# An attention loop with three turns in flight, its depthwise and output products in halves, and the next image's statistics beside qkv

## The chip, the core and the metric

The kernel runs on one core of one Trainium2 chip. The metric is the device time of one execution in microseconds (us). The engines are TensorE (PE: matmuls), VectorE (DVE), ScalarE (ACT), GpSimd (POOL) and SyncE (SP, which issues most transfers). Each engine runs its instructions in order; semaphores hold them together.

## The reference, cut to what matters

The kernel computes four layers on x of shape 8 x 128 x 56 x 56, each over a normalised input and added to it. The change touches only the first, attention over windows, once per image:

```python
xw = windows(x)                       # 7 x 7 windows of 8 x 8 pixels, 128 channels
proj = xw @ W_qkv + b_qkv             # q, k, v of 128 channels each
lepe = conv_general_dilated(v_img, lepe_w, padding='SAME', feature_group_count=C)  # 3 x 3 depthwise
logit = einsum('npc,nqc->npq', q_win * SCALE, k_win)      # window means
topk_logit, r_idx = top_k(logit, 4)
k_sel, v_sel = kv of the four chosen windows              # 256 keys for each window
attn = softmax(einsum('bmqc,bmkc->bmqk', q_h * SCALE, k_sel), axis=-1)   # 8 heads of 16
o = einsum('bmqk,bmkc->bmqc', attn, v_sel)
out = (o + lepe) @ W_o + b_o
```

## The kernel before

All images stay in SBUF (`X`). The eight images run one after the other (`B = 8`). For each, a qkv part makes q, k and v in seven blocks (`NBLK = 7`) of 448 pixels (`BLK`, 8 rows; `NWIN = 7` windows): ACT scales a block into `xb` (L1554), PE makes q, k, v and v by tokens (L1774 to L1782), ACT and DVE move them out of the banks, DVE sums windows (L1636). Then come the window logits, the search for the four best, and the transfer of the chosen indices (`row`, L1431). Depthwise blocks 0 and 1 run around the logits (L1800).

Then the attention loop over `P2 = 49` windows. In turn w the engines do, each in its order:

- PE (L1884 to L1888): `scores(w)` (L1829), four matmuls into banks 0 to 3, each waiting for the exponentials of the turn before (`s_ex`); `attend(w - 2)` (L1854), which waits for the copy `PT` (`s_Tc`), the gathered values (`s_vg`) and `s_o`; `turn(w - 1)` (L1842), eight transposes of the probabilities `Pr` into banks 4 and 5; `fill(w)`.
- ACT: `exps(w)` (L1567), `turned(w - 1)` (L1576), the copy to `PT`, and `fourth(w)`, the transfer of one of four value windows.
- DVE (L1722 to L1732): `maxes(w)` (L1666), the reciprocal of the first two sums (L1726), `between(w)`, the second reciprocal (L1729), and the fourth pair's normalising (L1731). `between(w)` holds `attended(w - 2)` (L1696, L1687), which joins the heads, and in some turns one more piece.
- POOL: `window(w + 2)` (L1494), the gather of keys, then `norm_first(w)` (L1504), the normalising of three pairs.
- SP: three of four value windows for each w (L1369), and `stack`, which lays rows for the depthwise product (L1398).

`fill(w)` on PE and `between(w)` on DVE share bank 7. The order is written out by hand in tables (L1299 to L1305). For block b: depthwise steps `lepe(b, dx)` at turns 7(b-2)+6, +7, +8; DVE's `copy_lepe(b)` (L1677) at 7(b-2)+9; the output product `out(b)` (L1811) at 7(b+1)+3; the output addition `add_out(b)` (L1671) at 7(b+1)+4 and `out_stats(b)` (L1682) a turn later. `out(b)` waits for `s_le` of block b+2, that is, for the copy; `lepe(b)` waits for `s_ev` of block b-3, that is, for the addition. The next image's statistics (`input_stats`, L1316) stand in turns 13, 15, 20, 22, 27, 29 and 30, and its mean and variance go over bank 7 in turns 33 and 40 (L1325, L1339, L1335).

```python
LEPE_AT = {NWIN * (b - 2) + 6 + dx: (b, dx) for b in range(2, NBLK) for dx in range(3)}
COPY_AT = {NWIN * (b - 2) + 9: b for b in range(2, NBLK)}
for w in range(2, P2):
    scores(w, w % 2)
    attend(w - 2, w % 2, (w - 2) % 3, (w - 2) // 3)
    turn(w - 1, (w + 1) % 2)
    fill(w)
```

Of the kernel before, what the change touches and what calls it, by code (L numbers as in the profile page):

```python
# [27 lines left out]
ACT = mybir.ActivationFunctionType  # L28
ALU = mybir.AluOpType
AXX = mybir.AxisListType.X  # L30
# [1108 lines left out]
def program(nc, a, out, last_stage=4):  # L1139
    root = ExitStack()  # L1140
    with root:
# [87 lines left out]
        with ExitStack() as c0:  # L1229
            sb, _, sem = mk(c0)  # L1230
            s_ldx = [sem("first_image_loaded"), sem("images_loaded")]
# [56 lines left out]
            Pr = sb("Pr", [C, 2, PAIRS, KEYS])  # L1288
# [3 lines left out]
            nmx = sb("nmx", [C, 2, PAIRS])  # L1292
            den = sb("den", [C, 2, PAIRS])
            rden = sb("rden", [C, 2, PAIRS])
# [77 lines left out]
            with nc.Block() as block:  # L1372
                @block.sync
                def _(sp):
# [9 lines left out]
                    for n in range(1, B):  # L1384
                        sp.dma_start(X[:, n * HW:(n + 1) * HW], x_in[n]).then_inc(s_ldx[1], 16)
# [83 lines left out]
                def _(pool):  # L1469
# [12 lines left out]
                    with pool.Fori(0, B) as n:  # L1482
# [15 lines left out]
                        def norm_first(w, par):  # L1498

                            for i, pairs in enumerate((slice(0, 2), slice(2, 3))):  # L1500
# [3 lines left out]
                                pool.tensor_tensor(Pr[:, par, pairs, :], Pr[:, par, pairs, :],  # L1504
                                                   rden[:, par, pairs].unsqueeze(2).to_broadcast([C, k, KEYS]), ALU.mult)\
# [4 lines left out]
                        with pool.Fori(0, (P2 - 3) // 2) as k:  # L1510
                            window(k * 2 + 2, 0)
                            norm_first(k * 2, 0)
                            window(k * 2 + 3, 1)
                            norm_first(k * 2 + 1, 1)
# [7 lines left out]
                def _(act):  # L1522
# [20 lines left out]
                    with act.Fori(0, B) as n:  # L1543
# [17 lines left out]
                        def exps(w, par):  # L1561

                            if not isinstance(w, int):
                                act.wait_ge(s_T, n * P2 + w)
# [45 lines left out]
                def _(dve):  # L1610
# [21 lines left out]
                    def image(n, more):  # L1632
# [343 lines left out]
```

## Time and profile before

| | us |
|---|---|
| median of 3 runs (3899.26 to 3907.92) | 3900.28 |
| profiled execution, its own time | 3898.74 |
| its span | 3897.0 |

The page's first two parts: busy time of each engine over the span, and the span in 40 slices of 97.4 us, in tenths.

```profile
PE 3509.7 (90%) x30516; PEld 2922.8 (75%) x30516; DVE 2500.8 (64%) x6153; ACT 2177.0 (56%) x5985; POOL 1837.3 (47%) x2998
...
PE   6989898888889898969999999999999968779998
...
DVE  4868687777868686853333333333333389989998
ACT  4878787887878787844443333333333334345554
POOL 2747374655647474720003333333334457756665
```

The attention layer is the first 17 slices or so. In the timeline an answer's line gives start, duration, engine, line of the kernel, operation, what it writes and reads, and how many instructions were merged; the brackets hold the idle time ahead of it and what ended it. A matmul of f32 data has two records.

### The profile page before, as it was taken

Reading aid. Unit: us, or ns where it says so; the run is one execution under the profiler, and the core shown is the slowest. Engines: PE = TensorE matmul, PEld = TensorE weight load, DVE = VectorE, ACT = ScalarE, POOL = GpSimd, SP = SyncE. Lnnn points to the kernel's source line nnn. Section 1 sums busy time; section 2 is a strip of 40 time slices with the busy share of each in tenths; the row PEclk is TensorE's granted clock in tenths of the full one; section 3 lists DMA queues with packets and bytes.
Section 4 is the critical chain, followed back from the end, with each engine's and each line's share of the span. In section 5 each row is a group of like instructions: output and inputs, shape, how many; then the busy total and the mean of one; then the engine's idle time right before and its main releaser. Section 6 shows DMA issues by size and latency. Waiting matters only on the chain. (4 is left out here: it accounts for less than half of the span.)

```text
span 3897.0 us, 106851 instructions
## 1 busy us (share of the span) xinstructions
PE 3509.7 (90%) x30516; PEld 2922.8 (75%) x30516; DVE 2500.8 (64%) x6153; ACT 2177.0 (56%) x5985; POOL 1837.3 (47%) x2998
## 2 busy tenths in 40 slices
PE   6989898888889898969999999999999968779998
PEld 3555555555555555559999999999999967779888
DVE  4868687777868686853333333333333389989998
ACT  4878787887878787844443333333333334345554
POOL 2747374655647474720003333333334457756665
PEclk9999999999999999989999999999999979989999
DMA  6232222223131323211110000000012100000000
GB/s 214 63 96 71 88 78 90 76 63 97 53 111 51 110 56 103 64 65 48 48 49 0 0 0 0 0 0 0 0 33 64 43 10 1 1 19 28 34 34 34
DMA packets 202728, 194.25 MB, mean 50 GB/s; under 512 B 35728, under 2 KB 190992, under 8 KB 199312
## 3 DMA queue, kind: packets, MB, share of 16 engines
q1 hardware_dynamic: 171024, 177.08, 14.6%
q10 hardware_dynamic: 31360, 12.87, 1.2%
q8 instruction: 181, 2.97, 0.3%
q14 instruction: 163, 1.34, 0.1%
HBM read 123.24 MB, written 66.58 MB: 49 GB/s over the span
## 5 line engine op out<-in xcount | busy, mean ns | idle before, releaser
L196 PE MATMUL bank<-h,w_hh 128*128 128x128 f32 x8032 | 933.8, 275 | 0.0
L196 PEld LDWEIGHTS bank<-h,w_hh 128*128 128x128 f32 x8032 | 917.1, 192 | 0.0
L1567 ACT ACTIVATE Pr<-bank,nmx 128x256 f32<-128x256 f32 x1568 | 721.0, 472 | 191.5 <-DVE nmx L1666 187.9
L241 ACT ACTIVATE h<-bank,bg 128x128 f32<-128x128 f32 x1008 | 370.0, 367 | 818.7 <-PE bank L196 818.6
L1504 POOL TENSOR_TENSOR Pr<-Pr,rden 128x512 f32<-128x512 f32 (+1 forms) x784 | 660.5, 853 | 182.6 <-DVE rden L1726 135.8
L1666 DVE TENSOR_REDUCE nmx<-bank 128x1 f32<-128x256 f32 x1568 | 553.8, 414 | 96.5 <-PE bank L1829 92.5
L1494 POOL COPY kg<-kT 128x64 f32 x1568 | 303.1, 237 | 535.0 <-DMA row<-ix 299.6
L287 DVE SCALAR_TENSOR_TENSOR inp<-bank,b_in,tz 128x256 f32<-128x256 f32 x196 | 85.8, 479 | 697.5 <-ACT tz L224 697.5
L260 POOL CAST h_hi<-h 128x512 fp32r<-128x512 f32 x196 | 119.7, 611 | 685.6 <-ACT h L241 685.6
L1829 PE MATMUL bank<-kg,qT 32*128 32x256 f32 x3136 | 410.3, 440 | 31.1 <-POOL kg L1494 22.3
L1576 ACT ACTIVATE PT<-bank 128x512 f32<-128x512 f32 x784 | 428.1, 609 | 15.9 <-PE bank L1842 15.7
L1842 PE MATMUL bank<-ident,Pr 128*128 128x128 f32 x3136 | 435.9, 283 | 0.0
L1842 PEld LDWEIGHTS bank<-ident,Pr 128*128 128x128 f32 x3136 | 341.9, 142 | 82.7 <-issue 73.3
L1854 PE MATMUL bank<-PT,vg 128*32 128x128 f32 x6272 | 265.2, 280 | 134.2 <-ACT PT L1576 129.9
L1829 PEld LDWEIGHTS bank<-kg,qT 32*128 32x128 f32 x3136 | 216.0, 189 | 225.5 <-ACT Pr L1567 155.8
L1854 PEld LDWEIGHTS bank<-PT,vg 128*32 128x32 f32 x6272 | 164.7, 110 | 281.1 <-issue 174.3
L970 POOL TENSOR_TENSOR v_ring<-points,v_ring 128x896 fp32r<-128x896 f32 x128 | 291.2, 2296 | 175.5 <-ACT v_ring L1000 175.5
L1567 ACT ACTIVATION_READ_ACCUMULATOR Pr<-bank,nmx 128x1 f32 x1568 | 318.0, 203 | 0.0
L661 PE MATMUL bank<-v_ring,u_hi 128*128 128x392 f32 x768 | 267.5, 348 | 52.7 <-POOL v_ring L970 52.7
L263 POOL TENSOR_TENSOR h_lo<-h,h_hi 128x512 fp32r<-128x512 f32 x196 | 251.6, 1284 | 35.3 <-POOL h_hi L260 35.3
L662 PE MATMUL bank<-v_ring,u_hi 128*128 128x392 f32 x768 | 262.9, 342 | 0.0
L663 PE MATMUL bank<-v_ring,u_lo 128*128 128x392 f32 x768 | 261.8, 341 | 0.0
(253 smaller groups left out, 6600.1 us busy)
## 6 DMA issues: line engine op xcount, KB each, us to landing
v_rows<-v_padded SPq DMA_DIRECT2D x168, 232.0 KB, 3.3
vg<-v_windows SPq DMA_DIRECT2D x1176, 32.0 KB, 2.1
first_gates<-gate_sums SPq DMA_DIRECT2D x28, 512.0 KB, 2.6
gate_sums<-first_gates SPq DMA_DIRECT2D x28, 512.0 KB, 3.6
v_padded<-vpad SPq DMA_DIRECT2D x56, 232.0 KB, 2.3
X<-in_x SPq DMA_DIRECT2D x8, 1568.0 KB, 15.1
vg<-v_windows ACTq DMA_DIRECT2D x392, 32.0 KB, 2.2
x_backup<-X SPq DMA_DIRECT2D x8, 1568.0 KB, 6.0
```

Source lines behind the costliest of these rows:

```text
L196: ins = pe.matmul(bank[m][:, tt * COLS:(tt + 1) * COLS], w_hh[:, k, m * 128:(m + 1) * 128], prev[:, k, :], start=False, stop=(k == NH - 1) ...
L241: act.activation(h[:, 2 * q + tt, m, :], bank[m][:, tt * COLS:(tt + 1) * COLS], ACT.Tanh, bias=bg[:, 0, m:m + 1]).then_inc(s_h, 1)
L661: pe.matmul(ps, w[0], x[0], start=first, stop=False)
L970: pool.tensor_tensor(halves(v[:, q % 3, 1], h), halves(pts, h), halves(v[:, q % 3, 0], h).bitcast(F32), ALU.subtract).then_inc(s_lo, 1)
L1494: ins = pool.tensor_copy(kg[:, par, r * W2:(r + 1) * W2], kT[:, bass.ds(i * W2, W2)])
L1504: pool.tensor_tensor(Pr[:, par, pairs, :], Pr[:, par, pairs, :], rden[:, par, pairs].unsqueeze(2).to_broadcast([C, k, KEYS]), ALU.mult)\
L1567: act.activation(Pr[:, par, j, :], bank[j][:, 0:KEYS], ACT.Exp, bias=nmx[:, par, j:j + 1], accum_out=den[:, par, j:j + 1])\
L1576: act.activation(PT[:, par, i * 512:(i + 1) * 512], bank[4 + i][:], ACT.Copy)\
L1666: dve.tensor_reduce(nmx[:, par, j:j + 1], bank[j][:, 0:KEYS], AXX, ALU.max, negate=True)\
L1829: pe.matmul(bank[j][:, 0:KEYS], qT[32 * j:32 * j + 32, w, :], kg[32 * j:32 * j + 32, par, :], start=True, stop=True).then_inc(s_S, 1)
L1842: ins = pe.transpose(bank[4 + j // 2][:, (j % 2 * 2 + c) * C:(j % 2 * 2 + c + 1) * C], Pr[:, par, j, c * C:(c + 1) * C], ident[:])
L1854: ins = pe.matmul(bank[6][32 * j:32 * j + 32, 0:C], vg[:, slot, c, 32 * j:32 * j + 32], PT[:, par, (2 * j + c) * C:(2 * j + c + 1) * C], s ...
```

## The change

The attention loop gets one more turn in flight: `Pr`, `nmx`, `den` and `rden` become rings of three, PE attends w-3 and turns w-2 beside scores w, ACT copies w-2, DVE joins w-3. The 448-column depthwise and output products are cut into halves of 224 columns; `FILL_AT` gives each half its turn: output halves at 7(b+1)+3 and +4, depthwise halves at 7(b-2)+5, +6, +7, +8 (two) and +9. The copy moves to 7(b-2)+10 and `ADD_LAG` to 5. The next image's seven bn_stats move out of the loop, one behind each qkv block; its aggregate to turn 6, the mean's product to turn 40 and the variance's to 41, with DVE's parts a turn later each. The second image's load gets a semaphore of its own. Block 2's rows are stacked from window 2 on. Loops of POOL and ACT are unrolled by six for the rings of three.

```diff
-            s_ldx = [sem("first_image_loaded"), sem("images_loaded")]
+            s_ldx = [sem("first_image_loaded"), sem("second_image_loaded"), sem("images_loaded")]
...
-            Pr = sb("Pr", [C, 2, PAIRS, KEYS])
+            Pr = sb("Pr", [C, 3, PAIRS, KEYS])
...
-            OUT_LAG, ADD_LAG = 3, 4
-            STATS_AT = {13: 0, 15: 1, 20: 2, 22: 3, 27: 4, 29: 5, 30: 6}
-            MEAN_AT, VAR_AT = 33, 40
-
-            LEPE_AT = {NWIN * (b - 2) + 6 + dx: (b, dx) for b in range(2, NBLK) for dx in range(3)}
-            COPY_AT = {NWIN * (b - 2) + 9: b for b in range(2, NBLK)}
-            STACK_AT = {3: 2, 8: 3, 12: 4, 18: 5, 25: 6}
+            ADD_LAG = 5
+            MEAN_AT, VAR_AT = 40, 41
+
+            HALF = BLK // 2
+            FILL_AT = {w: [] for w in range(P2)}
+            for b in range(NBLK - 1):
+                for h in range(2):
+                    FILL_AT[NWIN * (b + 1) + 3 + h].append(("out", b, 0, h))
+            for b in range(2, NBLK):
+                for i, w in enumerate((5, 6, 7, 8, 8, 9)):
+                    FILL_AT[NWIN * (b - 2) + w].append(("lepe", b, i // 2, i % 2))
+            COPY_AT = {NWIN * (b - 2) + 10: b for b in range(2, NBLK)}
+            STACK_AT = {2: 2, 8: 3, 12: 4, 18: 5, 25: 6}
...
-                        window(P2 - 1, 0)
-                        norm_first(P2 - 3, 0)
-                        norm_first(P2 - 2, 1)
-                        norm_first(P2 - 1, 0)
+                        with pool.Fori(0, (P2 - 2) // 6) as k:
+                            for i in range(6):
+                                window(k * 6 + i + 2, i % 2)
+                                norm_first(k * 6 + i, i % 3)
...
+                            if not (isinstance(w, int) and w < 3):
+                                act.wait_ge(s_T, n * P2 + w - 1)
...
+                        def turn_window(w, i):
+                            exps(w, (i + 2) % 3)
+                            turned(w - 2, i % 2)
+                            fourth(w - 1, (i + 1) % 3)
...
+                            if more:
+                                if b == 0:
+                                    dve.wait_ge(s_ldx[1], 16)
+                                input_stats(dve, following(n), b)
...
-                            if w >= 2:
-                                attended(w - 2)
+                            if w >= 3:
+                                attended(w - 3)
...
+                            if more and w == NWIN - 1:
+                                dve.wait_ge(s_ldx[2], 16 * (B - 2))
                                 input_aggregate(dve, following(n))
-                            if more and w == MEAN_AT:
+                            if more and w == MEAN_AT + 1:
                                 input_mean(dve, following(n))
-                            if more and w == VAR_AT:
+                            if more and w == VAR_AT + 1:
                                 input_var(dve, following(n))
...
+                                ins = pe.matmul(to[STRIP * i:STRIP * i + STRIP, h * HALF:(h + 1) * HALF],
+                                                w_tap[:, dx * STRIPS + i, :],
+                                                vrow[:, b % 2, i, h * ROWS // 2:(h + 1) * ROWS // 2, dx:dx + W],
+                                                start=(dx == 0 and h == 0), stop=(dx == 2 and h == 1))
...
+                        def out(b, h):
+                            if h == 0:
+                                pe.wait_ge(s_o, n * P2 + (b + 1) * NWIN + 1)
+                                if b + 2 < NBLK:
+                                    pe.wait_ge(s_le, n * NBLK + b + 3)
+                                else:
+                                    pe.wait_ge(s_ev, n * NBLK + b + 1)
+                            ins = pe.matmul(bank[7][:, h * HALF:(h + 1) * HALF], w_o[:],
+                                            by_row(oT[:, b % 2, :])[:, h * ROWS // 2:(h + 1) * ROWS // 2],
+                                            start=(h == 0), stop=(h == 1))
...
+                            for what, b, dx, h in FILL_AT[w]:
+                                if what == "out":
+                                    if more and b == NBLK - 2 and h == 0:
+                                        pe.wait_ge(s_id, following(n) * IN_DVE + 4)
+                                    out(b, h)
+                                else:
+                                    if dx == 0 and h == 0:
+                                        if b == 2:
+                                            pe.wait_ge(s_le, n * NBLK + 2)
+                                        else:
+                                            pe.wait_ge(s_ev, n * NBLK + b - 1)
+                                    lepe(b, dx, h, bank[7])
                             if more and w in (MEAN_AT, VAR_AT):
-                                pe.wait_ge(s_ev, n * NBLK + b + 2)
+                                pe.wait_ge(s_ev, n * NBLK + (w - NWIN) // NWIN + 2)
...
-                        for w in range(2, P2):
+                        for w in range(3, P2):
                             scores(w, w % 2)
-                            attend(w - 2, w % 2, (w - 2) % 3, (w - 2) // 3)
-                            turn(w - 1, (w + 1) % 2)
+                            attend(w - 3, (w - 3) % 2, (w - 3) % 3, (w - 3) // 3)
+                            turn(w - 2, (w - 2) % 3)
                             fill(w)
```

## Rows read from the trace of the kernel before

**Rows 1.** The timeline (start us, us, engine, line, operation), DVE: marks of turns 0, 20, 27, 48.
```profile
275.00 0.17 DVE L1726 RECIPROCAL rden<-den 128x2 f32<-128x2 f32 x1
...
341.30 0.17 DVE L1726 RECIPROCAL rden<-den 128x2 f32<-128x2 f32 x1
...
364.78 0.17 DVE L1726 RECIPROCAL rden<-den 128x2 f32<-128x2 f32 x1
...
434.95 0.17 DVE L1726 RECIPROCAL rden<-den 128x2 f32<-128x2 f32 x1
```

**Rows 2.** The timeline, second image, turns 13 to 15, PE and ACT.
```profile
319.18 0.62 ACT L1576 ACTIVATE PT<-bank 128x512 f32<-128x512 f32 x1
...
320.05 0.67 PE L1854 MATMUL bank<-PT,vg 128*32 128x128 f32 x16 [0.28 <-ACT PT L1576]
...
321.67 0.96 PE L1800 MATMUL bank<-v_rows,w_tap 96*32 96x448 f32 x8
...
322.56 0.71 PE L1829 MATMUL bank<-kg,qT 32*128 32x256 f32 x8
...
323.75 0.47 ACT L1567 ACTIVATE Pr<-bank,nmx 128x256 f32<-128x256 f32 x1 [0.60 <-DVE nmx L1666]
...
325.56 0.61 ACT L1576 ACTIVATE PT<-bank 128x512 f32<-128x512 f32 x1
```

**Rows 3.** The timeline, second image, turns 9 and 10.
```profile
303.83 0.47 ACT L1567 ACTIVATE Pr<-bank,nmx 128x256 f32<-128x256 f32 x1 [0.81 <-DVE nmx L1666]
...
305.59 0.61 DVE L1677 COPY lepe<-bank 128x448 f32<-128x448 f32 x1
...
307.03 0.47 ACT L1567 ACTIVATE Pr<-bank,nmx 128x256 f32<-128x256 f32 x1 [0.30 <-DVE nmx L1666]
...
308.31 0.92 PE L1811 MATMUL bank<-oT,w_o 128*128 128x448 f32 x2
```

**Rows 4.** Idle time by releaser (us, times): PE ahead of L1842, PE ahead of L1854.
```profile
  POOL Pr L1504: 9.4, 29
...
  ACT PT L1576: 231.5, 445
```

**Rows 5.** The timeline, end of the second image's loop.
```profile
435.71 1.09 ACT L1576 ACTIVATE PT<-bank 128x512 f32<-128x512 f32 x2
...
436.86 0.67 PE L1854 MATMUL bank<-PT,vg 128*32 128x128 f32 x16 [1.25 <-ACT PT L1576]
...
438.59 1.08 ACT L1576 ACTIVATE PT<-bank 128x512 f32<-128x512 f32 x2 [1.78 <-PE bank L1842]
```

**Rows 6.** The timeline, marks of turns 0, 1 and 2 of the third image.
```profile
483.40 0.17 DVE L1726 RECIPROCAL rden<-den 128x2 f32<-128x2 f32 x1
...
486.43 0.17 DVE L1726 RECIPROCAL rden<-den 128x2 f32<-128x2 f32 x1
...
490.14 0.17 DVE L1726 RECIPROCAL rden<-den 128x2 f32<-128x2 f32 x1
```

**Rows 7.** Busy time by stretch; the third number from the end is the granted clock.
```profile
486.00:488.00 2.00, 2.00 (x15) 1.56 (x13) 1.13 (x5) 1.82 (x8) 1.77 (x6) 0.50 0.16 44
```

**Rows 8.** The timeline: output addition, input statistics, then the mean in turn 33.
```profile
312.09 0.68 DVE L1671 SCALAR_TENSOR_TENSOR X<-bank,cb,X 128x448 f32 x1
...
318.63 0.62 DVE L1316 BATCH_NORM_STATS2 bn_in<-X 128x6 f32 x1
...
384.21 0.47 ACT L1567 ACTIVATE Pr<-bank,nmx 128x256 f32<-128x256 f32 x1 [0.23 <-DVE nmx L1666]
...
385.76 0.28 PE L1325 MATMUL bank<-input_norm,group 128*128 128x1 f32 x2
...
386.85 0.22 DVE L1335 SCALAR_TENSOR_TENSOR input_norm<-input_norm 128x1 f32<-128x1 f32 x1
```

**Rows 9.** The timeline, DVE in a qkv block before the third image's loop.
```profile
459.25 0.68 DVE L1642 TENSOR_SCALAR kT<-bank,vec 128x448 f32<-128x448 f32 x1 [1.52 <-PE bank L1775]
```

**Rows 10.** The images' loads from in_x: time from issue to landing.
```profile
DMA to landing us min/median/max: 6.7/15.1/26.3
```

More of the change, by code:

```diff
@@ L1509, in _ @@
                         window(1, 1)
[L1510 to L1514, printed above, removed]
-                        window(P2 - 1, 0)
-                        norm_first(P2 - 3, 0)
-                        norm_first(P2 - 2, 1)
-                        norm_first(P2 - 1, 0)
+                        with pool.Fori(0, (P2 - 2) // 6) as k:
+                            for i in range(6):
+                                window(k * 6 + i + 2, i % 2)
+                                norm_first(k * 6 + i, i % 3)
+                        for w in range((P2 - 2) // 6 * 6, P2):
+                            if w + 2 < P2:
+                                window(w + 2, w % 2)
+                            norm_first(w, w % 3)
                     pool.wait_ge(s_S, (B * P2 + 1) * PAIRS)
@@ L1599, in _ @@
                         exps(0, 0)
-                        with act.Fori(0, (P2 - 1) // 6) as k:
-                            for i in range(6):
-                                exps(k * 6 + i + 1, (i + 1) % 2)
-                                turned(k * 6 + i, i % 2)
-                                fourth(k * 6 + i + 1, (i + 1) % 3)
-                        turned(P2 - 1, 0)
+                        exps(1, 1)
+                        def turn_window(w, i):
+                            exps(w, (i + 2) % 3)
+                            turned(w - 2, i % 2)
+                            fourth(w - 1, (i + 1) % 3)
+                        exps(2, 2)
+                        turned(0, 0)
+                        fourth(1, 1)
+                        with act.Fori(0, (P2 - 3) // 6) as k:
+                            for i in range(1, 7):
+                                turn_window(k * 6 + i + 2, i)
+                        for w in range((P2 - 3) // 6 * 6 + 3, P2):
+                            turn_window(w, w - 2)
+                        turned(P2 - 2, (P2 - 2) % 2)
+                        fourth(P2 - 1, (P2 - 1) % 3)
+                        turned(P2 - 1, (P2 - 1) % 2)
                         with act.If(n < B - 1):
@@ L1792, in image, with lepe @@
                         pe.wait_ge(s_v, n * NBLK + NBLK)
-                        def lepe(b, dx, to):
-                            if dx == 0:
+                        def lepe(b, dx, h, to):
+                            if dx == 0 and h == 0:
                                 loads = 4 - b % 2
@@ L1814, in image @@
-                        for dx in range(3):
-                            lepe(0, dx, bank[7])
+                                ins = pe.matmul(to[STRIP * i:STRIP * i + STRIP, h * HALF:(h + 1) * HALF],
+                                                w_tap[:, dx * STRIPS + i, :],
+                                                vrow[:, b % 2, i, h * ROWS // 2:(h + 1) * ROWS // 2, dx:dx + W],
+                                                start=(dx == 0 and h == 0), stop=(dx == 2 and h == 1))
+                            if dx == 2 and h == 1:
+                                ins.then_inc(s_lp, 1)
@@ L1816, in image @@
+                        for i in range(6):
+                            lepe(0, i // 2, i % 2, bank[7])
                         pe.wait_ge(s_k, n * NBLK + NBLK)
@@ L1818, in image @@
                         pe.matmul(bank[1][0:P2, 0:P2], qs[:], ks[:], start=True, stop=True).then_inc(s_lg, 1)
-                        for dx in range(3):
-                            lepe(1, dx, bank[6])
+                        for i in range(6):
+                            lepe(1, i // 2, i % 2, bank[6])
                         pe.wait_ge(s_tk, n * 3 + 2)
@@ L1830, in scores, with turn @@
                                           start=True, stop=True).then_inc(s_S, 1)
-                        def turn(w, par):
+                        def turn(w, tri):
                             pe.wait_ge(s_nF, (n * P2 + w) * 2 + 1)
```

81 lines of the change are left out of this document (29 added, 52 removed).

## The prediction

> **What bounds the kernel now.** I read the page's first two parts, then how one line that runs once per turn is spaced, then one image's loop in order of time. Per image there are 49 windows, one turn each: PE writes scores, DVE takes maxima, ACT exponentiates, POOL and DVE normalise, PE turns the probabilities, ACT copies them, PE attends. DVE's first reciprocal (L1726) marks the turn. In the second image the marks run from 275.00 to 434.95: 48 turns in 159.95 us [rows 1]. All that is changed lies in this first stage, eight images long.
>
> No engine is full in the loop, so I look for rings of waits. E(w) is the start of ACT's exponentials of turn w.
>
> Ring one goes over two turns [rows 2]: a copy to PT ends at 319.80, attend starts at 320.05 (+0.25), the fill behind attend and turning at 321.67 (+1.62), the next scores at 322.56 (the fill, +0.89), exponentials at 323.75 (+1.19), the next copy at 325.56 (+1.81), and it takes 1.09 [rows 5]. The first step is 0.06 where a copy starts at 435.71 and attend at 436.86 [rows 5]; the mean I take is 0.18. Without its fill the ring is 0.18 + 1.62 + 1.19 + 1.81 + 1.09 = 5.89: E(w+1) is not before E(w-1) + 5.89 + the fill of turn w.
>
> Ring two goes over one turn, between ACT and DVE: exponentials at 303.83 and 307.03, 3.20 apart, where DVE has a depthwise copy of 0.61 in the turn [rows 3]. I take 3.2 also for turns with an output addition (0.68) or output statistics (0.62, as the row of the input's), [rows 8]. Without such work it is 3.03 (marks 483.40 and 486.43) [rows 6].
>
> With d(w) = E(w+1) - E(w): d(w) is the larger of ring two and 5.89 + fill - d(w-1). Turns 20 to 26 come out at 3.58, 3.2, 3.58, 3.2, 3.53, 3.2, 3.2 = 23.5; measured 364.78 - 341.30 = 23.48 [rows 1]. The two rules carry the loop.
>
> **Three turns in flight.** PE's order was scores(w), attend(w-2), turning(w-1); it becomes scores(w), attend(w-3), turning(w-2). ACT's was exponentials(w), copy(w-1); it becomes exponentials(w), copy(w-2). Before and after, PE in turn w waits for the copy that ACT made in turn w-1, and ACT in turn w copies what PE turned in turn w. Both rings keep their steps and lengths. What gets a turn more room is the normalising, between exponentials and turning, and it has room now: PE waited 9.4 us for POOL's probabilities in the whole kernel, 29 times in 392 turns [rows 4]. I take nothing for it; 9.4 is the most.
>
> The deeper loop drains longer. A stage of attend, turning and copy takes 2.9 us (copies start at 435.71 and 438.59 [rows 5]), and there is one more: +2.9 per image. At the start turn 1 takes 3.71 now (486.43 to 490.14 [rows 6]), since turning(0) stands ahead of scores(2); it moves behind, and ring two alone is left: 3 x 3.03 = 9.1 for turns 0 to 2, some 0.8 less. But TensorE's granted clock there is 0.50, the 1.2 GHz level [rows 7], after a stretch with little work, and the new order has still less work for PE at that place, so a turn more may run at it: bounds 0 and +1.4 (turning, attend and scores at twice their time, less what ring two hides); I take +0.6, between them, as nothing decides.
>
> **Halves.** A depthwise step of 448 columns adds 0.89; its row says 0.96, so the end overlaps by 0.07, and the output product's 0.92 [rows 3] adds 0.85. A half adds at least half: 0.445 and 0.42. It is eight records of 224 columns. Scores' eight of 256 take 0.71, attend's sixteen of 128 take 0.67, with the same 32-column weights as here [rows 2]. By scores a half is 0.61; by a straight line between attend (0.042 less the overlap) and the full step (0.111) it is 0.48. I take 0.48 and 0.44 for the weights' form. The Trainium skill would have it near the lower end: "TensorE: Matmul & The Clock Gate", section on the back-to-back issue gap, has a gap of columns over clock and some 2.5 ns, so a cut costs next to nothing; by that the sum is some 6 us less, and no row here has such a half.
> In seven turns there were four fills, 3.5 us; there are eight halves, 3.76, two of them in one turn. Were that all, turns would even out to 3.34, 3.2, 3.17, 3.68, 3.03, 3.30, 3.03 = 22.75 for 23.5.
>
> **The new waits.** Here the change hurts. In the kernel before each buffer goes from DVE to PE with a turn between: lepe(2) is copied by DVE in turn 9 (305.59), output product 0 runs on PE in turn 10 (308.31) [rows 3]. After the change the copy of block b is at 7(b-2)+10, and the output product of block b-2, which waits for it (s_le) as both use bank 7, at 7(b-1)+3: the same number. Likewise the first depthwise step of block 3 is in turn 12 and waits (s_ev) for output addition 0, which ADD_LAG 5 puts in turn 12. DVE comes to this work 1.76 after E(w) and ends at +2.37 (copy) or +2.44 (addition) [rows 3, 8]; PE is ready at +1.28 (308.31 for E = 307.03 [rows 3]). PE runs in order: behind the waiting fill stand scores(w+1), and behind those DVE's maxima and ACT. So d = 2.37 + 0.1 + 0.44 + 1.19 = 4.1 with a copy and 2.44 + 0.1 + 0.48 + 1.19 = 4.2 with an addition, 0.1 being the wake-up (between 0.06 and 0.25 above). Copies fall on turns 10, 17, 24, 31, 38, additions on 12, 19, 26, 33: nine turns per image. A period is 4.2 + 3.2 + 3.17 + 3.68 + 3.03 + 4.1 + 3.03 = 24.4, for 23.5.
>
> **The next image's statistics.** Seven bn_stats of 0.62 [rows 8] leave the loop for the qkv blocks, one each. There DVE idles 1.52 per block behind PE's k product [rows 9], so 0.9 is left over; where DVE starts an image late it has made that up after two blocks. I take 0; if the cover fails, 7 x 0.6 per image. DVE's wait for image 1 stands ahead of the first image's window sums and so of ACT: issued at 7.0 as the first of seven, landing 6.7 to 26.3 later [rows 10], likely before qkv starts, at worst some 10 us once.
> The mean's product moves from turn 33 to 40, where PE must first wait for output addition 4, in turn 40 as well: 2.44 + 0.1 + 0.2 + 1.19 = 3.93, 0.2 being the product (0.28 in its row). The variance's product in turn 41 waits for the mean's chain, which ends 2.86 after E (384.21, 386.85 + 0.22): 2.86 + 0.1 + 0.2 + 1.19 = 4.35 [rows 8].
> Depthwise blocks 0 and 1 are in halves too. Block 0 stands ahead of the logits: 6 x 0.48 for 3 x 0.89, +0.2; block 1 lies beside the search for the four best and their transfer. SP stacks block 2's rows a window earlier and PE wants them a turn earlier; the last goes out behind window 3's gathers, two turns ahead of its use. SP's gathers and ACT's fourth keep their distance to attend. Nothing for these.
>
> **The sum, an image with a next one.** Turns 0 to 4: 9.1 + 3.6 + 3.0 = 15.7. Turns 5 to 11: 3.34, 3.03, 3.34, 3.51, 3.03, 4.1, 3.03 = 23.4. Turns 12 to 39: 4 x 24.4 = 97.6. Turns 40 to 47: 3.93, 4.35, 3.15, 3.03, 3.03, 3.30, 3.03, 3.2 = 27.0. Together 163.7 for 159.95: +3.8. Drain +2.9, block 0 +0.2: +6.9, seven times: +48. The last image has neither statistics nor the waits of the norm, before or after; I put it at +6. In all +54 us on the profiled execution's 3898.74: 3953 us. The median of the runs stands 1.5 above that execution, which I leave to the range.
>
> **The rivals.**
> *A, the waits are met (the other side: faster).* If DVE's copy or addition is done when PE comes to the fill, the nine turns fall back to 3.3 (-7.5) and the two of the norm to 3.2 (-1.9): -2.5 per image with the drain, 3880 us in all. It decides at one point: whether PE reaches the fill earlier or later than 2.4 after E(w). It is there at 1.28, so against it. Partly met (3893 to 3906) is no change.
> *B, the third turn takes away PE's wait ahead of attend.* PE idled 231.5 us there behind ACT's copy [rows 4]. A gap that repeats can come from too few buffers, and then turns would fall to ring two's 3.03: 48 x 3.03 = 145.4, +3.1, so -11.4 per image, some 3807 us. Against it: what ends this gap is ACT's copy of the turn before, in the new order as in the old. (The Trainium skill, "Perfetto Trace Analysis", section on the optimization strategy, reads consistent bubbles so.)
> *C, halves at the scores' rate, 0.61.* +0.13 for each of four waiting fills, half of that for some 20 others, 0.8 on block 0: +2.6 per image, 3974 us.
> *D, the low clock lasts* a turn more at the start and falls in the longer drain, where turning and attend then take twice their time: +2 per image, 3970 us.
>
> **How the numbers follow.** Forecast 0.64; A 0.06, partly met 0.06; B 0.03; C 0.11; D 0.10. Low end: each wait 0.2 cheaper (9 x 8 x 0.2 = 14) and no slow turn at the start (5): 3932. High end: C with half of D: 3985. Left out are A, B and their like, 0.15, and little above. The measurement can tell 0.2%, 8 us, from no change. Faster 0.09 (A, B), same 0.06, slower 0.85.
>
> **What would show it.** The marks L1726 4.1 to 4.2 apart in turns 10, 12, 17, 19, 24, 26, 31, 33 and 38, 3.9 in 40, 4.4 in 41, and 3.0 to 3.2 in most others; PE idle ahead of the output product and the first depthwise half, ended by DVE's copy and addition; three copies after the last exponentials; blocks of qkv no longer than before. It is wrong if those turns take 3.3, or the others fall well below 3.0 or rise above 3.4.

## The result

| | before | after |
|---|---|---|
| median of 4 runs each, us | 3900.13 (3899.26 to 3907.92) | 3968.29 (3965.46 to 3972.22) |
| profiled execution, its own time | 3898.74 | 3965.46 |
| its span | 3897.0 | 3963.6 |
| loop, turn 0 to turn 48, mean of images 0 to 6 | 159.99 | 164.29 |
| loop of the last image | 156.15 | 160.07 |
| last mark to the next image's first, mean of seven | 48.11 | 51.77 |

The ratio is 1.0171, 95% interval 1.0153 to 1.0189: slower, by 68 us where 54 were forecast. A mark is, as before, DVE's first reciprocal of a turn; it stands in L1744 now. "Turn w" is from mark w to mark w+1. The loops and gaps in this table and in all that follow are worked out from the 392 marks of a trace.

The span's +66.6 splits so: seven loops 7 x 4.30 = 30.1, the last loop 3.9, seven gaps 7 x 3.67 = 25.7, the first mark 0.9 later (68.12 for 67.23), 3.1 between the last mark and the next layer's first product L196, and 2.9 behind it, where the change touches nothing.

The page's first part: no engine got much more work.

```profile
PE 3521.4 (89%) x31972; PEld 2970.5 (75%) x31972; DVE 2482.8 (63%) x6153; ACT 2180.1 (55%) x5985; POOL 1831.1 (46%) x2998
```

PE has 12 us more busy time and DVE 18 us less than before. So most of the 68 us is not added work; it comes from the order. The timeline of the second image, turns 10 and 12 (start us, us, engine, line, operation, what it writes and reads; in brackets the idle time ahead of it and what ended it):

```profile
315.98 0.47 ACT L1572 ACTIVATE Pr<-bank,nmx 128x256 f32<-128x256 f32 x1
...
317.66 0.61 DVE L1698 COPY lepe<-bank 128x448 f32<-128x448 f32 x1
...
318.42 0.62 PE L1833 MATMUL bank<-oT,w_o 128*128 128x224 f32 x2 [0.55 <-DVE lepe L1698]
...
318.97 0.82 PE L1854 MATMUL bank<-kg,qT 32*128 32x256 f32 x8
...
320.16 0.47 ACT L1572 ACTIVATE Pr<-bank,nmx 128x256 f32<-128x256 f32 x1 [1.17 <-DVE nmx L1687]
...
323.11 0.47 ACT L1572 ACTIVATE Pr<-bank,nmx 128x256 f32<-128x256 f32 x1
...
324.77 0.68 DVE L1692 SCALAR_TENSOR_TENSOR X<-bank,cb,X 128x448 f32 x1
...
325.58 0.59 PE L1819 MATMUL bank<-v_rows,w_tap 96*32 96x224 f32 x8 [0.57 <-DVE X L1692]
...
327.28 0.47 ACT L1572 ACTIVATE Pr<-bank,nmx 128x256 f32<-128x256 f32 x1 [1.15 <-DVE nmx L1687]
```

In turn 10 the exponentials start at 315.98 and the next ones at 320.16: 4.18. One follows the chain through four engines. DVE ends the copy at +2.29, PE starts the output half at +2.44, scores at +2.99, and the next exponentials start at +4.18. Behind PE's 0.55 us of waiting ACT idles 1.17 for DVE's maxima: a wait on one engine is handed round. In the kernel before, the same product had the turn to itself [rows 3] and scores didn't wait. Turn 12 is the same with the addition and the first depthwise half, 4.17.

The groups by line tell how often over the whole kernel (busy us, mean ns, then the idle time ahead and what ended it):

```profile
L1819 PE MATMUL bank<-v_rows,w_tap 96*32 96x224 f32 x2688 | 172.0, 360 | 24.9 <-DVE X L1692 20.5 <-ACT vst L1543 4.5
...
L1833 PE MATMUL bank<-oT,w_o 128*128 128x224 f32 x224 | 66.9, 389 | 33.8 <-DVE lepe L1698 27.9 <-DVE oT L1708 5.9
```

The rows hold what is new: 20.5 us ended by the addition and 27.9 by the copy. The view of L1833 puts the 27.9 down to 40 waits, five copies in each of eight images.

Turn 41 of the same image, where the variance's product waits for the mean's chain:

```profile
426.59 0.22 DVE L1341 SCALAR_TENSOR_TENSOR input_norm<-input_norm 128x1 f32<-128x1 f32 x1
...
426.87 0.38 PE L1345 MATMUL bank<-input_norm,group 128*128 128x1 f32 x2 [1.48 <-DVE input_norm L1341]
...
428.37 0.47 ACT L1572 ACTIVATE Pr<-bank,nmx 128x256 f32<-128x256 f32 x1 [1.43 <-DVE nmx L1687]
```

This wait has a second price, in some images only. In the first, third and seventh image TensorE's granted clock falls to the 1.2 GHz level right behind it, and turn 42 takes 4.02 to 4.06 us where it takes 2.95 in the other four with a next image. The third image, PE behind the variance's product, and the windows around it (the third number from the end is the granted clock):

```profile
643.97 0.38 PE L1345 MATMUL bank<-input_norm,group 128*128 128x1 f32 x2 [1.40 <-DVE input_norm L1341]
...
646.14 1.97 PE L1867 MATMUL bank<-ident,Pr 128*128 128x128 f32 x8
```

```profile
642.00:644.00 2.00, 0.60 (x7) 0.36 (x5) 1.79 (x9) 2.00 (x8) 1.43 (x4) 1.00 0.11 31
...
646.00:648.00 2.00, 2.00 (x12) 1.57 (x8) 1.68 (x8) 1.41 (x7) 1.68 (x6) 0.50 0.06 16
```

The eight transposes take 1.97 us there; in the second image, with the same wait of 1.48 and the clock at 1.00, they take 1.09.

The end of the loop (its last mark is 448.19), which answers to [rows 5], and the first two qkv blocks of the next image:

```profile
450.32 0.67 PE L1879 MATMUL bank<-PT,vg 128*32 128x128 f32 x16 [1.49 <-ACT PT L1581]
...
456.26 0.67 PE L1879 MATMUL bank<-PT,vg 128*32 128x128 f32 x16 [1.38 <-ACT PT L1581]
...
461.57 1.86 PE L1793 MATMUL bank<-PT,w_qkv 128*128 128x448 f32 x2 [2.05 <-ACT PT L1559]
...
463.23 1.70 PE L1794 MATMUL bank<-PT,w_qkv 128*128 128x448 f32 x2
...
466.21 1.87 PE L1801 MATMUL bank<-w_qkv,PT 128*128 128x128 f32 x8
...
468.01 1.02 PE L1793 MATMUL bank<-PT,w_qkv 128*128 128x448 f32 x2
```

Three attends behind the last mark (the first and the last are shown) where there were two: the last starts 8.07 us after it, before 4.98 (439.93 after the mark at 434.95, [rows 1]). That is +3.09. And in this gap the whole first qkv block runs at the 1.2 GHz level: its four products take 6.44 us (461.57 to 468.01), where the one before had its third and fourth at full rate, 1.15 and 1.19, and took 5.25 (445.22 to 450.47). The windows show the clock:

```profile
456.00:458.00 2.00, 1.01 (x17) 0.77 (x18) 0.89 (x4) 1.49 (x3) 0.00 (x0) 0.87 0.01 4
458.00:460.00 2.00, 1.52 (x4) 0.83 (x3) 1.21 (x7) 0.53 (x1) 0.00 (x0) 0.50 0.05 12
...
466.00:468.00 2.00, 2.00 (x9) 1.40 (x7) 0.39 (x1) 0.00 (x0) 0.00 (x0) 0.57 0.04 17
...
500.00:502.00 2.00, 1.19 (x5) 1.19 (x6) 1.32 (x5) 1.80 (x8) 1.12 (x5) 0.50 0.13 36
...
510.00:512.00 2.00, 2.00 (x22) 1.62 (x15) 1.68 (x7) 1.89 (x8) 1.40 (x5) 0.50 0.06 16
512.00:514.00 2.00, 1.27 (x19) 0.73 (x21) 1.39 (x5) 1.26 (x3) 1.13 (x3) 0.98 0.17 48
```

By these shares the first low stretch runs from about 457.5 to 467.7, after a drain in which PE was idle for nearly half of the time, and the second to 512.1, past the mark of turn 3 (511.01). The seven gaps differ: the first qkv block takes 4.99 to 6.44 us (mean 5.99), where it took 4.93 to 5.29 (mean 5.12) before.

### The profile page after: what moved, and what is told of

Same layout as the page of the kernel before. It is cut to its first block and busy times, and to the rows that moved or that the text cites. A ratio compares the mean times of both kernels' runs of the same rounds, so it can differ in the third digit from the quotient of the medians.

```text
span 3963.6 us, 108732 instructions
## 1 busy us (share of the span) xinstructions
PE 3521.4 (89%) x31972; PEld 2970.5 (75%) x31972; DVE 2482.8 (63%) x6153; ACT 2180.1 (55%) x5985; POOL 1831.1 (46%) x2998
## 3 DMA queue, kind: packets, MB, share of 16 engines
q8 instruction: 194, 3.18, 0.3%
## 5 line engine op out<-in xcount | busy, mean ns | idle before, releaser
L196 PE MATMUL bank<-h,w_hh 128*128 128x128 f32 x8032 | 933.8, 275 | 0.0
L196 PEld LDWEIGHTS bank<-h,w_hh 128*128 128x128 f32 x8032 | 917.0, 192 | 0.0
L1510 POOL TENSOR_TENSOR Pr<-Pr,rden 128x512 f32<-128x512 f32 (+1 forms) x784 | 658.2, 853 | 157.6 <-DVE rden L1744 140.1
L1854 PE MATMUL bank<-kg,qT 32*128 32x256 f32 x3136 | 380.2, 448 | 34.5 <-POOL kg L1500 22.1
L1854 PEld LDWEIGHTS bank<-kg,qT 32*128 32x128 f32 x3136 | 199.2, 192 | 172.6 <-ACT Pr L1572 86.1
```

The source lines that it names most:

```text
L196: ins = pe.matmul(bank[m][:, tt * COLS:(tt + 1) * COLS], w_hh[:, k, m * 128:(m + 1) * 128], prev[:, k, :], start=False, stop=(k == NH - 1) ...
L1510: pool.tensor_tensor(Pr[:, tri, pairs, :], Pr[:, tri, pairs, :], rden[:, tri, pairs].unsqueeze(2).to_broadcast([C, k, KEYS]), ALU.mult)\
L1854: pe.matmul(bank[j][:, 0:KEYS], qT[32 * j:32 * j + 32, w, :], kg[32 * j:32 * j + 32, par, :], start=True, stop=True).then_inc(s_S, 1)
```

## The experiments

Each kernel was timed in several rounds beside the kernel before on the same chip, in four groups: the kernel before came out at 3900.13, 3904.02, 3901.60 and 3901.53. So when times of different groups are set side by side, up to 4 us can be the group's. All results in one table (loop and gap as above; "period" is turns 12 to 18, the sum of their medians over images 0 to 6; "in flight" the turns). Loops and gaps are of the one profiled execution, which lies up to 5.9 us off its kernel's median (x6_cut and x5_two 5.9 and 5.3 above, x1_gaps and x3_sooner 5.4 and 5.0 below):

| kernel | in flight | us | beside before | ratio (95%) | loop | period | gap |
|---|---|---|---|---|---|---|---|
| before | 2 | | | | 159.99 | 23.48 | 48.11 |
| after | 3 | 3968.29 | 3900.13 | 1.0171 (1.0153 to 1.0189) | 164.29 | 24.29 | 51.77 |
| x1_gaps | 3 | 3920.43 | 3904.02 | 1.0043 (1.0026 to 1.0060) | 158.49 | 23.03 | 51.79 |
| x2_addgap | 3 | 3958.83 | 3904.02 | 1.0137 (1.0120 to 1.0154) | 163.32 | 24.05 | 51.61 |
| x3_sooner | 3 | 3924.46 | 3904.02 | 1.0053 (1.0036 to 1.0070) | 159.00 | 23.28 | 51.91 |
| x4_three | 3 | 3928.14 | 3904.02 | 1.0060 (1.0043 to 1.0077) | 159.29 | 23.40 | 52.34 |
| x8_undo3 | 2 | 3952.54 | 3901.60 | 1.0126 (1.0108 to 1.0144) | 165.52 | 24.95 | 49.28 |
| x6_cut | 2 | 3900.88 | 3901.60 | 1.0000 (0.9990 to 1.0009) | 160.38 | 23.49 | 48.38 |
| x7_stats | 2 | 3904.14 | 3901.60 | 1.0012 (1.0003 to 1.0022) | 159.87 | 23.48 | 48.22 |
| x5_two | 2 | 3894.13 | 3901.60 | 0.9978 (0.9968 to 0.9988) | 158.96 | 23.13 | 49.07 |
| x9_late | 2 | 3893.76 | 3901.53 | 0.9977 (0.9968 to 0.9986) | 158.15 | 23.12 | 48.73 |
| x10_both | 3 | 3911.46 | 3901.53 | 1.0022 (1.0013 to 1.0031) | 157.61 | 23.03 | 51.42 |

### The waits: x1_gaps, x2_addgap, x3_sooner

The theory: the nine turns of 4.2 come from hand-overs over bank 7 that DVE and PE have in the same turn. Three ways to take them away, each on the kernel after.

x1_gaps gives each hand-over its turn again, with all else kept:

```diff
-            ADD_LAG = 5
+            ADD_LAG = 4
-                    FILL_AT[NWIN * (b + 1) + 3 + h].append(("out", b, 0, h))
+                    FILL_AT[NWIN * (b + 1) + 3].append(("out", b, 0, h))
-                for i, w in enumerate((5, 6, 7, 8, 8, 9)):
+                for i, w in enumerate((5, 6, 6, 7, 7, 8)):
-            COPY_AT = {NWIN * (b - 2) + 10: b for b in range(2, NBLK)}
+            COPY_AT = {NWIN * (b - 2) + 9: b for b in range(2, NBLK)}
```

> The changed kernel with a turn between every hand-over of bank 7: depthwise halves in turns +5, +6, +6, +7, +7, +8, copy at +9, both output halves in one turn, addition a turn later; three turns in flight and the statistics beside qkv stay. Theory (the nine same-turn waits): no turn of 4.18 is left but turn 41; a period of seven turns falls from 24.3 to 23.2, the mean's wait goes, 6 us less per image: about 3920 us. Rival (the time comes from the third turn, the halves or the clock, not from the waits): the time stays at 3968.

x2_addgap takes away the additions' four alone; the copies' five stay:

```diff
-                for i, w in enumerate((5, 6, 7, 8, 8, 9)):
+                for i, w in enumerate((6, 6, 7, 8, 8, 9)):
```

> The changed kernel with only the first depthwise half a turn later (turns +6, +6, +7, +8, +8, +9): the four waits for the output addition go, the five for the copy stay. Theory: turns 12, 19, 26, 33 fall from 4.17 to 3.2, turns 10, 17, 24, 31, 38 stay at 4.18; a period falls by 0.6 as the halves crowd in two turns; about 3950 us. Rival: no change, 3968.

x3_sooner keeps the tables and turns DVE's order round, so that the copy or addition is ready earlier:

```diff
-                            if w >= 3:
-                                attended(w - 3)
                             b, lag = divmod(w - NWIN, NWIN)
                             if w in COPY_AT:
                                 copy_lepe(COPY_AT[w])
                             if b >= 0 and lag == ADD_LAG:
                                 add_out(b)
+                            if w >= 3:
+                                attended(w - 3)
```

> The changed kernel with DVE doing the copy or the addition before the two attended steps of the same turn, so that it ends 0.54 us sooner after the exponentials; all tables as they are. Theory (PE waits for DVE's piece in the same turn): the nine turns of 4.18 and turn 40 each fall by 0.54, 5.4 per image, about 3925 us. Rival: the same work in another order on DVE, no change, 3968.

The groups of the depthwise and output products by line, first x1_gaps, then x2_addgap, then x3_sooner:

```profile
L1819 PE MATMUL bank<-v_rows,w_tap 96*32 96x224 f32 x2688 | 163.7, 359 | 5.1 <-ACT vst L1543 5.1
...
L1833 PE MATMUL bank<-oT,w_o 128*128 128x224 f32 x224 | 52.9, 359 | 5.9 <-DVE oT L1708 5.9
```

```profile
L1819 PE MATMUL bank<-v_rows,w_tap 96*32 96x224 f32 x2688 | 163.7, 359 | 6.0 <-ACT vst L1543 6.0
...
L1833 PE MATMUL bank<-oT,w_o 128*128 128x224 f32 x224 | 64.9, 378 | 32.1 <-DVE lepe L1698 26.2 <-DVE oT L1708 5.9
```

```profile
L1819 PE MATMUL bank<-v_rows,w_tap 96*32 96x224 f32 x2688 | 172.0, 360 | 9.0 <-ACT vst L1543 4.2 <-DVE X L1692 3.6
...
L1833 PE MATMUL bank<-oT,w_o 128*128 128x224 f32 x224 | 64.9, 378 | 12.4 <-DVE lepe L1698 6.0 <-DVE oT L1708 5.9
```

In x1_gaps both kinds of wait are gone, and with them the mean's in turn 40 (3.96 to 3.09), and so are 48 of the 68 us (3920.43; 52, each kernel beside its own kernel before). Turn 41 is 4.27, no other median over 3.8. In x2_addgap "DVE X" is gone and "DVE lepe" stays at 26.2, in the places foretold: turns 12, 19, 26 and 33 fell from 4.17 to 3.17 to 3.40, turns 10, 17, 24, 31 and 38 kept 4.18. But the time fell by 9 us only (13, each beside its own kernel before): turns 13 and 15 rose from 3.09 and 3.61 to 3.76 and 3.92. What a turn is spared is partly paid in the next ones, as ring one goes over two turns. A small part is the clock: the low stretch behind turn 41 comes in six images of x2_addgap (turn 42 at 3.41 to 4.04) and in three of the kernel after, some 2 us more. So the kinds don't add up: the nine together with the mean's wait are worth 48 us, the four alone 9.

In x3_sooner the work is the same in the same turns, only 0.6 us earlier. Its turn 10, in the second image:

```profile
310.12 0.17 DVE L1744 RECIPROCAL rden<-den 128x2 f32<-128x2 f32 x1
...
310.20 0.62 DVE L1698 COPY lepe<-bank 128x448 f32<-128x448 f32 x1
...
310.97 0.62 PE L1833 MATMUL bank<-oT,w_o 128*128 128x224 f32 x2
...
313.76 0.17 DVE L1744 RECIPROCAL rden<-den 128x2 f32<-128x2 f32 x1
```

The copy starts 0.08 after the mark for 0.62, the output half 0.85 for 1.38, and the turn takes 3.64 for 4.18: what the copy gains, the turn gains. Turn 41, whose wait is not touched, stays at 4.33. So the length of these turns hangs on when DVE is done.

### Three turns in flight: x4_three, x8_undo3

x4_three has three in flight alone: whole products in the old turns (the copy at +9, ADD_LAG 4), the statistics in the loop as before. x8_undo3 is the other way round, the kernel after with two in flight:

```diff
-                            attend(w - 3, (w - 3) % 2, (w - 3) % 3, (w - 3) // 3)
-                            turn(w - 2, (w - 2) % 3)
+                            attend(w - 2, w % 2, (w - 2) % 3, (w - 2) // 3)
+                            turn(w - 1, (w + 1) % 2)
```

> The kernel before with three turns in flight alone: whole products, the old tables, statistics in the loop. Theory: the loop's turns stay as before, each image pays the longer drain (+3.1) and some 1.5 of low clock behind it: about 3928 us. Rival (the third turn takes away PE's wait ahead of attend): well below 3900.

> The changed kernel without its third turn: rings of two, attend w-2, turning w-1, but the changed tables with their same-turn waits, halves and statistics beside qkv. Theory (third turn worth +24 to +29, waits the rest): the turns of 4.18 stay, the drain is one stage shorter; about 3941 us. Rival (the third turn softens the waits): above 3968.

x4_three is +24 us beside its kernel before, as foretold. The first and last of the three attends in its drain (last mark 437.30), and the wait ahead of attend in its whole kernel:

```profile
439.50 0.67 PE L1878 MATMUL bank<-PT,vg 128*32 128x128 f32 x16 [1.49 <-ACT PT L1582]
...
445.43 0.67 PE L1878 MATMUL bank<-PT,vg 128*32 128x128 f32 x16 [1.38 <-ACT PT L1582]
```

```profile
  ACT PT L1582: 240.3, 457
```

The gap from image to image is 4.2 us longer, the loop 0.7 shorter. Of the 4.2 the drain is 3.1: in every gap of all kernels with three in flight the last attend starts 8.04 to 8.13 us behind the last mark, with two in flight 4.97 to 5.00. The first qkv block adds 0.7 (mean 5.82 for 5.12). PE's wait for PT is 240.3 us, for 231.5 [rows 4]: a third buffer does nothing for a bubble that ends with the copy of the turn before.

x8_undo3 came out at 3952.54, 11 over the 3941 expected: taking three in flight away gives back some 17 us of 68 (16 by the medians alone), and the waits cost no less with two turns in flight: the loop is even 1.2 longer. The nine turns are 4.24 to 4.26 there. The expectation had the loop unchanged by the turns in flight; in all four pairs (x4_three with before, after with x8_undo3, x10_both with x9_late and with x5_two) three in flight shortens it, by 0.7, 1.2, 0.5 and 1.3 us per image, and lengthens the gap, by 4.2, 2.5, 2.7 and 2.4. In the last three pairs the gap grows by less than the drain's 3.1: their kernels with two in flight have longer first qkv blocks (means 5.74, 5.80 and 5.73) than the kernel before (5.12). Why the low clock falls otherwise there was not found. Which wait the third turn relieves was not found: PE's wait for POOL's probabilities is 9.4 us before and 10.4 in x4_three.

### The cut and the statistics alone: x6_cut, x7_stats

x6_cut is the kernel before with every product in two halves, both in the turn of the whole one:

```diff
+            for b in range(NBLK - 1):
+                for h, w in enumerate((3, 3)):
+                    FILL_AT[NWIN * (b + 1) + w].append(("out", b, 0, h))
+            for b in range(2, NBLK):
+                for i, w in enumerate((6, 6, 7, 7, 8, 8)):
+                    FILL_AT[NWIN * (b - 2) + w].append(("lepe", b, i // 2, i % 2))
```

> The kernel before with every depthwise and output product cut in two, both halves in the old turn. Theory from the changed kernel's rows (two halves back to back take 0.90 for 0.89): the cut itself costs nothing, 3901 to 3906 us. Rival (a half at 0.48 alone, or at the scores' rate 0.61): 3910 to 3950.

3900.88, ratio 1.0000, and a period of 23.49 for 23.48: the cut costs nothing. The timeline of the kernel after shows why (last image: one half, the scores behind it, and in the next turn two halves):

```profile
1699.35 0.59 PE L1819 MATMUL bank<-v_rows,w_tap 96*32 96x224 f32 x8
...
1699.87 0.71 PE L1854 MATMUL bank<-kg,qT 32*128 32x256 f32 x8
...
1702.44 0.96 PE L1819 MATMUL bank<-v_rows,w_tap 96*32 96x224 f32 x16
```

Two halves one behind the other take 0.90 (1702.44 to the next scores at 1703.34), the whole step took 0.89 [rows 2]; a half alone delays scores by 0.52; why that is more than half of the whole was not run apart. The Trainium skill, "TensorE: Matmul & The Clock Gate", section on the back-to-back issue gap, gives the gap between isolated matmuls at the full clock as columns over the clock and some 2.5 ns. By that a cut costs next to nothing, an estimate from the page's figure, and for halves that stay together the run agrees: 3900.88 for 3901.60.

x7_stats is the kernel before with the statistics alone moved: seven bn_stats into the qkv blocks, the mean's product in turn 40, the variance's in 42.

```diff
-            STATS_AT = {13: 0, 15: 1, 20: 2, 22: 3, 27: 4, 29: 5, 30: 6}
-            MEAN_AT, VAR_AT = 33, 40
+            MEAN_AT, VAR_AT = 40, 42
```

> The kernel before with only the next image's statistics moved beside qkv, and its mean's and variance's products in turns 40 and 42, each with a turn between. Theory: qkv's blocks stay at 3.48, turns 30, 33 and 35 of the loop fall from 3.7 to 3.1, so 1.9 less per image: about 3890 us. Rival (the cover in qkv fails): 7 x 0.6 more per image, 3920 or more.

The expectation was wrong: 3904.14, ratio 1.0012, for 3890. The cover in qkv held (the gap is 48.22 for 48.11), but the loop is 0.12 shorter, not 1.9. By the medians, turns 13, 15, 20, 22, 27 and 29, from which a bn_stats had gone, did not move by more than 0.01: what DVE did there had held up nothing. Turns 30 and 33 gained (3.74 to 3.21, 3.69 to 3.18), but turn 31 rose from 2.95 to 3.31 and turn 34 from 3.03 to 3.48; the sums of turns 26 to 32 and 33 to 39 are 0.16 and 0.18 lower, and that of 40 to 47 is 0.31 higher. Turn 41 shows by what:

```profile
412.62 0.17 DVE L1726 RECIPROCAL rden<-den 128x2 f32<-128x2 f32 x1
...
413.32 0.15 DVE L1329 COPY input_norm<-bank 128x1 f32<-128x1 f32 x1
...
414.06 0.22 DVE L1334 SCALAR_TENSOR_TENSOR input_norm<-input_norm 128x1 f32<-128x1 f32 x1
...
414.51 0.17 DVE L1729 RECIPROCAL rden<-den 128x2 f32<-128x2 f32 x1 [0.23 <-issue]
...
416.48 0.17 DVE L1726 RECIPROCAL rden<-den 128x2 f32<-128x2 f32 x1
```

The mean's three steps (the first and the last are shown) stand between the two reciprocals, 413.32 to 414.28, and the second one comes 1.89 after the first. The turn is 3.86.

### What is left: x5_two, x9_late, x10_both

x5_two is two in flight with all the rest: halves in the old order but spread (5, 6, 6, 7, 7, 8), statistics in qkv, products of the norm in turns 40 and 42.

> Two turns in flight, halves spread with a turn between every hand-over (+5, +6, +6, +7, +7, +8, copy +9, output in one turn, addition a turn later), statistics beside qkv, norm in turns 40 and 42. Theory: what is good in the change without what costs; a period of seven turns 23.15 for 23.5 and 1.9 for the statistics, 3.5 less per image: about 3875 us. Rival (spreading halves brings nothing): as the statistics alone, 3890.

3894.13, ratio 0.9978: faster than the kernel before, but by 7 us, not by 26. Its period is 23.13, where the cut alone has 23.49 and the statistics alone 23.48: the 0.35 come from the halves' spread over more turns, or from that and the lighter DVE together; the spread wasn't run by itself. Turn 41 is 3.86 as in x7_stats, and turn 2 is 4.38 in five of the first seven images, where it is 3.03 and 3.21 in the other two. In such an image (mark of turn 0 at 691.29) the low clock is still there in turn 2:

```profile
698.00:700.00 2.00, 2.00 (x12) 1.67 (x15) 1.40 (x5) 1.16 (x6) 1.64 (x3) 0.50 0.28 99
```

x10_both is x1_gaps with the variance's product in turn 42 for 41, which makes it x5_two with three turns in flight. x9_late is x5_two with the two products in 41 and 43:

```diff
-            MEAN_AT, VAR_AT = 40, 42
+            MEAN_AT, VAR_AT = 41, 43
```

> Two turns in flight, halves in the old order and statistics in qkv, as in the run with two in flight that took 3894; only the products of the next image's mean and variance stand in turns 41 and 43 for 40 and 42. There, turn 41 took 3.86 us, with the mean's three DVE steps behind the output statistics. Theory, the pieces of DVE crowd in one turn: apart from each other no turn near 40 to 44 is over 3.4, some 0.5 us less per image, 3890 us. Rival, the chain of the mean costs its turn wherever it stands: a turn of 3.8 or more reappears in 42 or 44, 3894 us or more.

> Three turns in flight with halves, statistics in qkv and a turn between every hand-over of bank 7 (the run of 3920 us), and the variance's product a turn later (42 for 41), so that it too has a turn between. Theory, the last 4.27 us turn goes to 3.3 to 3.9: 3 to 7 us less, 3914 to 3917 us. Then three in flight is still 20 to 24 us slower than two with all else the same, since what it costs is the drain and the low clock behind it. Rival, most of the surplus of 3920 over the kernel before was that one wait: under 3905 us.

x9_late took 3893.76 for 3894.13, no difference that can be told. Turn 41 fell from 3.86 to 3.00 and turn 42 rose from 3.03 to 3.61: the rival was right that the chain lengthens the turn where it stands, though 3.61 is less than the 3.8 it named. The expectation misplaces the output statistics: in x5_two they stand in turn 40 (408.48 in the second image), not beside the mean's steps (411.66). (The profiled execution of x9_late, 3889.32, lies below its median and that of x5_two, 3899.44, above, so their loops and gaps differ by more than their times.)

x10_both took 3911.46, 9 less than x1_gaps (6.5, each beside its own kernel before) for 3 to 7 expected, turn 41 at 3.54 for 4.27. Its PE no longer waits ahead of the variance's product, and the low stretch behind turn 41, which x1_gaps has in three images, comes in none: turn 42 is 2.95 to 2.96 in all seven images with a next one. It differs from x5_two by three in flight alone and is 17.3 us behind it. Beside x9_late, where the norm's products stand a turn elsewhere, it is 17.7 behind: seven gaps 2.7 longer are 18.8, and the last drain adds 2.9, less eight loops 0.5 shorter, 4. So in the best setting found three turns in flight still lose.

## Why the prediction was right, step by step

**The two rings and the waits.** They carried the forecast. The turns, as medians of images 0 to 6:

| turn | forecast | measured |
|---|---|---|
| 10, 17, 24, 31, 38 (copy) | 4.1 | 4.18 each |
| 12, 19, 26, 33 (addition) | 4.2 | 4.16 to 4.17 |
| 40 (mean) | 3.93 | 3.96 |
| 41 (variance) | 4.35 | 4.33 |
| period, turns 12 to 18 | 24.4 | 24.29 |
| loop with a next image | 163.7 | 164.29 |

By these medians no other turn from 4 on is over 3.7; what they hide is turn 42, 4.0 in three of the seven images. In the copy's turn the steps were forecast as 2.37 + 0.1 + 0.44 + 1.19 and measured as 2.29 + 0.15 + 0.55 + 1.19.

**The halves.** 0.48 and 0.44 were taken; alone they delay scores by 0.52 and 0.55, a pair by 0.90 in all. The bounds held both. Rival C, 0.61 for each, did not come: block 0 with its six steps took 2.41 us on PE (490.64 to 493.05, 48 records) for 2.39 before (473.33 to 475.72, 24 records), where C had +0.8 and the sum +0.2.

**The start and the clock.** Turns 0 to 4 were put at 15.7, with +0.6 between bounds of 0 and +1.4, and took 16.56, so it was the high end. Turn 2 is 3.61 in all eight images and turn 3 anything from 2.96 to 4.38 (3.69, 2.96, 3.87, 4.38, 2.96, 2.96, 4.10, 3.44), by how long the clock stays low. That is rival D's first half, +0.8 per image in the mean (16.47).

**The loop's sum, and luck in it.** Against the forecast's 163.7 turns 0 to 4 are +0.8, turns 5 to 39 -0.7 (each period 0.1 to 0.2 shorter) and turns 40 to 47 +0.5, nearly all of it from turn 42 in the three images. That last term had no place in the sum: the forecast had the variance's wait itself right, 4.35 for 4.33, but put nothing for what the wait does to the clock behind it. That the loop comes out at +0.6 is errors of both signs that partly cancel.

**The drain.** +2.9 was forecast and 3.09 measured in the second image. The gap grew by 3.67 in the mean (+3.1 with block 0 was forecast), by the drain's 3.1 and 0.9 of the first qkv block, less 0.3 elsewhere. It grew by 4.61 ahead of the third image (448.19 to 501.25 for 434.95 to 483.40 [rows 1, 6]): 3.09 for the drain, 1.2 for the first qkv block and 0.5 for the first scores (1.24 for 0.71), both at 1.2 GHz, less 0.2 elsewhere. D had the drain's own turning and attend slowed; they ran at full rate (attend 0.67 three times), and what stands behind them was slowed.

**Three in flight in the loop.** The forecast took nothing for it; the runs have a gain of 0.5 to 1.3 us per image. Rival B fell: PE's wait ahead of attend stayed (240 us in x4_three). The Trainium skill, "Perfetto Trace Analysis", section on the optimization strategy, says that consistent bubbles can mean too few buffers. Here they didn't: one more turn of buffers left the bubble as it was, and its drain and what follows cost 24 us.

**The statistics.** Their cover in qkv held: DVE's idle time ahead of kT fell from 1.52 [rows 9] to 0.99 with a bn_stats of 0.62 in it, and a block is 3.48 long as before (474.98 to 478.46 between two q products). DVE's wait for the second image's load cost nothing that shows.

**The waits' price, seen from rival A.** A's mechanism was answered by x3_sooner: where the copy is ready 0.56 earlier, the turn is 0.54 shorter. But its 3880 was too low. Without the nine waits and the mean's the kernel is at 3920 (x1_gaps) and, without the variance's, at 3911 (x10_both). A's loop, 163.7 less 9.4, is 154.3; x10_both has 157.6. One failed term is 22.75 for a period without waits: it is 23.03 to 23.10, which over four periods is 1.3 of the 3.3. The rest is 0.7 in turns 0 to 4, 0.6 in turns 5 to 11, and 0.7 in turns 40 to 47, where turn 41 is 3.54 and not 3.2. The nine waits cost 4.9 us per image in turns 5 to 39 (120.3 in the kernel after, 115.4 in x1_gaps), not 7.5. The nine turns themselves are 0.7 to 1.0 longer, 7.4 together (turn 10 is 3.48 in x1_gaps, turn 19 3.33), and the turns behind them shorter (turn 11 2.95 for 3.15, turn 13 3.09 for 3.53). The forecast of the kernel after didn't need these terms, the rival did.

**The rest of the miss,** 12 us of 66.6 in the span: loops +3.5 (7 x 0.5, the remainder of the sum above), gaps +4.0, the last image +1, the first mark +0.9, and 2.9 in layers that the change doesn't touch, for which the forecast had no step and no run has a reason.

## What to carry to other kernels

In a loop like this one, two in-order engines that hand a buffer over want a turn between the two ends. With both ends in the same turn every engine in the ring waited, though the work had not grown. Before adding a stage in flight, ask what ends the bubble it is to fill. Here it was the work of the turn before, and the deeper loop brought a longer drain, once for every time that the loop ends. And moving work out of a loop gives back only what that work held up: the bn_stats of x7_stats had held up nothing in six of their seven turns.

## What was not expected of the hardware

What follows a drain can cost more than the drain, through the clock. Ahead of the third image's qkv part the granted clock was 0.50 for some 6.8 us in the kernel before (442.0 to 448.8, by the shares of its windows) and 10.2 in the kernel after, and the first qkv block ran at 1.2 GHz to its end: 1.70 us for a product of 448 columns that takes 0.92 at 2.4 GHz, 1.87 for eight of 128 that take 1.19. At the start of the loop it was 6.8 and 13.6 us. But this is no rule for three in flight: the same block takes anything from 4.99 to 6.44 us in the seven gaps of the kernel after, 4.86 to 6.38 in x10_both, and 4.89 to 6.42 with two in flight (x9_late), while the drain itself is 3.1 longer every time.

A wait inside the loop can lower the clock as well. All five kernels with the variance's product in turn 41, where PE waits 1.2 to 1.6 us for the mean's chain, have images with a short low stretch right behind it (the kernel after 3, x1_gaps 3, x2_addgap 6, x3_sooner 2, x8_undo3 2, of seven each), and turn 42 is then up to 1.2 us longer. The seven kernels without that wait have none; one of them, x10_both, differs from x1_gaps only in this product's turn. The waits of 0.55 us for the copies and the additions are followed by none anywhere.

How long the low level lasts is not set by the code alone. The same turn 3 takes 2.96 to 4.38 us in the eight images of one execution, and with two turns in flight the same turn 2 takes 3.03 to 4.38 (x5_two) where it is 3.06 to 3.32 in the kernel before. So a few us of each comparison above, and part of the 2.4 to 4.2 per gap among them, are the clock's and not the order's; what decides between a short and a long stretch was not found.
